# Ternary weights turned by a transposing DMA, and their scales spread over the partitions through a line in DRAM

## What is computed

```
q    = x + braak_embed[stage][..., None]            # (16, 256, 256)
attn = softmax(einsum('bsd,btd->bst', q, f))
y    = einsum('bst,btd->bsd', attn, f)              # the kernel uses attn @ (f @ H)
xh   = y @ H                                        # H: Hadamard, 256 x 256
s    = clip(max|xh| over a row, 1e-05) / 7
xq   = clip(round(xh / s), -8, 7) * s
ws   = clip(mean|weight| over a row, 1e-05)         # one scale for each of 256 outputs
tern = +1 where weight/ws > 0.5, -1 where < -0.5, else 0
out  = x + einsum('bsi,oi->bso', xq, tern * ws)
```

## Time and profile before

| | |
|---|---|
| median of 3 runs | 108.36 us (107.94 to 108.78) |
| the profiled execution: its time | 108.61 us |
| its span in the trace | 106.8 us |
| mean granted clock of PE | 0.97 |
| PE busy | 97.4 us, 91% |
| DVE busy | 87.7 us, 82% |
| ACT busy | 76.1 us, 71% |
| POOL busy | 47.1 us, 44% |
| DMA queue of SP and ACT, share of 16 engines | 45.1% |

### The profile page before, as it was taken

How to read it: one execution, slowest core, us unless ns; L and a number is a source line. 1 busy time by engine, 2 the same in 40 slices (tenths; PEclk the granted TensorE clock), 3 DMA queues, 4 the chain that set the end, 5 groups by cost and what they waited for, 6 DMA issues and landing times.

```text
span 106.8 us, 2584 instructions
## 1 busy us (share of the span) xinstructions
PE 97.4 (91%) x799; PEld 90.9 (85%) x799; DVE 87.7 (82%) x216; ACT 76.1 (71%) x200; POOL 47.1 (44%) x66
## 2 busy tenths in 40 slices
PE   5969899999999999999999999999999998995640
PEld 2439799899999999999999999999999998995410
DVE  1085699798989898989989898989898989699880
ACT  3255986969696978787878787878788865780610
POOL 5034699404343435343435353535353534058050
PEclk9999999999999999999999999999999999999855
DMA  3984632425253664947282728282722222202214
GB/s 68 256 298 120 257 112 30 169 53 199 49 173 134 175 215 119 228 111 237 96 227 86 245 68 262 54 289 49 292 51 98 49 98 49 98 0 98 98 53 143
DMA packets 14850, 14.71 MB, mean 138 GB/s; under 512 B 8054, under 2 KB 8956, under 8 KB 14844
## 3 DMA queue, kind: packets, MB, share of 16 engines
q1 hardware_dynamic: 14688, 14.62, 45.1%
q10 hardware_dynamic: 156, 0.01, 0.1%
HBM read 8.73 MB, written 4.19 MB: 121 GB/s over the span
## 4 chain that ended last, share of the span: by engine, by line
PE 72%; DVE 14%; ACT 4%; DMA 3%; issue 3%; ACTq 1%; DVEq 0%
PE score_bank L461 19%; PE xh_bank L461 18%; PE fh_bank L461 12%; PE prob_bank L450 6%; PE out_bank L516 5%; PE f_bank L450 5%; PE q_bank L450 5%; DMA stage_of<-itok_dram 3%; ACT prob L672 2%; DVE prob_lo L841 1%; DVE least_scale L863 1%; DVE fh_lo L841 1%; DVE raw_scale L819 1%; DVE xh_bank L996 1%; DVE result L1002 1%
## 5 line engine op out<-in xcount | busy, mean ns | idle before, releaser
L359 POOL TENSOR_TENSOR result<-scaled,x_all 128x512 f32<-128x512 f32 x13 | 16.7, 1281 | 24.3 <-DVE scaled L827 24.3
L351 POOL TENSOR_TENSOR code<-code,magic 128x512 bf16<-128x512 f32 x13 | 13.5, 1040 | 14.8 <-ACT code L650 14.8
L650 ACT ACTIVATE code<-xh_bank,inv_scale 128x256 f32<-128x256 f32 x30 | 12.8, 486 | 4.8 <-DVE inv_scale L953 2.8
L672 ACT ACTIVATE prob<-score_bank,neg_max 128x256 f32<-128x256 f32 x32 | 15.0, 478 | 0.9 <-DVE neg_max L868 0.9
L841 DVE TENSOR_TENSOR prob_lo<-prob_bank,prob_hi 128x512 fp32r<-128x512 f32 x16 | 11.1, 691 | 5.2 <-ACT prob_hi L662 5.2
L666 ACT CAST fh_hi<-fh_bank 128x512 fp32r<-128x512 f32 x16 | 9.4, 589 | 7.9 <-PE fh_bank L461 7.7
L461 PE MATMUL score_bank<-f_hi,q_hi 128*128 128x256 f32 x64 | 14.1, 302 | 0.3 <-ACT prob L672 0.3
L461 PE MATMUL fh_bank<-had,f_hi 128*128 128x256 f32 x64 | 14.0, 299 | 0.0
L641 ACT CAST f_hi<-f_bank 128x512 fp32r<-128x512 f32 x15 | 8.8, 587 | 5.7 <-PE f_bank L450 5.7
L461 PE MATMUL score_bank<-f_lo,q_hi 128*128 128x256 f32 x64 | 12.8, 282 | 0.0
L461 PE MATMUL score_bank<-f_hi,q_lo 128*128 128x256 f32 x64 | 12.8, 282 | 0.0
(11 more groups left out here) (129 smaller groups left out, 232.5 us busy)
## 6 DMA issues: line engine op xcount, KB each, us to landing
f_nat<-f_dram SPq DMA_DIRECT2D x16, 256.0 KB, 2.8
x_all<-x_dram SPq DMA_DIRECT2D x16, 256.0 KB, 3.0
out_dram<-result SPq DMA_DIRECT2D x14, 256.0 KB, 2.0
out_dram<-result SPq DMA_DIRECT2D x4, 128.0 KB, 1.8
w_raw<-weight_dram SPq DMA_DIRECT2D x1, 256.0 KB, 4.8
code_t<-code SPq DMA_TRANSPOSE x13, 2.5
had_block<-hadamard_dram SPq DMA_DIRECT2D x1, 64.0 KB, 3.9
embed_sb<-embed_dram ACTq DMA_DIRECT2D x1, 6.0 KB
```

The source lines that it names most:

```text
L351: nc.gpsimd.tensor_tensor(as_rows(code16[:, b.k]), as_rows(code), magic[:, :].broadcast_to([P, W]), ALU.subtract).then_inc(code16_ready, 1)
L359: nc.gpsimd.tensor_tensor(result[:, b.k], as_rows(scaled[:, b.k]), x_all[:, b.at], ALU.add).then_inc(result_ready, 1)
L650: return nc.scalar.activation(to[:, t], xh[:, t], ACT.Copy, bias=MAGIC, scale=inv_scale[:, b.k, t:t + 1])
L672: a = nc.scalar.activation(prob[:, t], score_bank[:, t], ACT.Exp, bias=neg_max[:, b.k, t:t + 1], accum_out=row_sum[:, b.k, t:t + 1])
```

## The change

Both ways of the weight over PE are removed, and with them `ones`, `w_diag`, the two DVE copies and the four waits around them. In their place:

- `tern` is stored by POOL in the order chunk, tile, column, so that one transposing DMA (128 x 512, bf16, as for the codes) gives `tern_t`. POOL still does it in one instruction; its output now goes to four runs of 128 elements.
- `w_scale` (128 x 2, fp32) is stored to a line of 256 elements in DRAM, element by element, and SP waits for its landing; a second DMA then reads the line into all 128 partitions as `w_scale_row`.
- All three stand in SP's queue in front of its step 3, that is behind the loads of batch 4, and in front of the loads of batch 5 and of the turning of the codes of batch 0.
- PE waits for `tern_t` before its step 4 as before, no longer for the row; DVE waits for the row before its step 4.

```
 @@ SP
+            def weight_row():
+                sp.wait_ge(w_scale_ready, 1)
+                sp.dma_start(w_scale_line.rearrange("(t p) -> p t", p=P), w_scale[:, :],
+                             allow_slow_non_contiguous=True
+                             ).then_inc(line_stored, 16)
+                sp.wait_ge(line_stored, 16)
+                sp.dma_start(w_scale_row[:, :], w_scale_line.partition_broadcast(P)
+                             ).then_inc(row_ready, 16)
+
+            def turn_weights():
+                sp.wait_ge(tern_ready, 1)
+                sp.dma_start_transpose(tern_t[:, :, :].rearrange("p c (t s) -> p (c t) s", t=T),
+                                       tern[:, :, :, :].rearrange("p c t d -> p (c t d)")
+                                       ).then_inc(tern_t_ready, 16)
+
             for i in range(B + LAG_STORE - 2):
+                if i == LAG_QUANT:
+                    weight_row()
+                    turn_weights()
                 step(peeled(i), dma_turns=i - LAG_QUANT < turned_by_dma)
 @@ POOL
-            nc.gpsimd.memset(ones[:, :], 1.0).then_inc(ones_ready, 1)
...
-                nc.gpsimd.tensor_tensor(tern[:, :, :], w_pos[:, :, :], w_neg[:, :, :], ALU.subtract
-                                        ).then_inc(tern_ready, 1)
+                nc.gpsimd.tensor_tensor(tern[:, :, :, :].rearrange("p c t d -> p t c d"),
+                                        w_pos[:, :, :].rearrange("p t (c d) -> p t c d", c=C),
+                                        w_neg[:, :, :].rearrange("p t (c d) -> p t c d", c=C),
+                                        ALU.subtract).then_inc(tern_ready, 1)
 @@ PE
-            def weights():
-                pe.wait_ge(tern_ready, 1)
-                for c in range(C):
-                    for t in range(T):
-                        pe.transpose(tern_half[:, c, t * P:(t + 1) * P],
-                                     tern[:, t, c * P:(c + 1) * P], ident16[:, :])
-                pe.wait_ge(diag_ready, 1)
-                pe.wait_ge(ones_ready, 1)
-                for t in range(T):
-                    mm = pe.matmul(out_bank[:, 0, t * P:(t + 1) * P], ones[:, :], w_diag[:, t],
-                                   start=True, stop=True)
-                mm.then_inc(weights_in_bank, 1)
...
-                    if stage == times_hadamard:
-                        weights()
                     stage(b)
-            pe.wait_ge(tern_t_ready, 1)
-            pe.wait_ge(row_ready, 1)
+            pe.wait_ge(tern_t_ready, 16)
 @@ ACT
-            act.wait_ge(w_scale_ready, 1)
-            for t in range(T):
-                a = nc.scalar.activation(w_diag[:, t], ident[:, :], ACT.Copy, scale=w_scale[:, t:t + 1])
-            a.then_inc(diag_ready, 1)
 @@ DVE
-            def weight_copies():
-                dve.wait_ge(weights_in_bank, 1)
-                nc.vector.tensor_copy(tern_t[:, :, :], tern_half).then_inc(tern_t_ready, 1)
-                nc.vector.tensor_copy(w_scale_row[:, :], out_bank[:, 0]).then_inc(row_ready, 1)
...
-                    if stage == split_fh:
-                        weight_copies()
                     stage(b)
+            dve.wait_ge(row_ready, 16)
             for i in range(4, 2 * LOOP_FROM):
```

More of the change, by code:

```diff
@@ L71, in adaln_ffn_kernel @@
         warm = sb("warm", [P, W], BF16)
-        ones = sb("ones", [P, P], F32)
         had_block = sb("had_block", [P, P], F32)
@@ L82, in adaln_ffn_kernel @@
         w_pos = sb("w_pos", [P, T, D], F32)
-        tern = sb("tern", [P, T, D], BF16)
+        tern = sb("tern", [P, C, T, P], BF16)
         tern_t = sb("tern_t", [P, C, O], BF16)
-        w_diag = sb("w_diag", [P, T, P], F32)
         w_scale_row = sb("w_scale_row", [P, O], F32)
+        w_scale_line = nc.dram_tensor("w_scale_line", [O], F32, kind="Internal").ap()
         stage_of = sb("stage_of", [P, B], I32)
@@ L133, in adaln_ffn_kernel @@
         out_bank = bank("out_bank", [P, T, O], F32)
-        tern_half = out_bank[:, T - 1].bitcast(BF16).rearrange("p (c o) -> p c o", c=C)
         last_xh_banks = [f_bank, q_bank]
@@ L171, in adaln_ffn_kernel @@
         bias_ready = sem("bias_ready")
-        ones_ready = sem("ones_ready")
         had_ready = sem("had_ready")
@@ L179, in adaln_ffn_kernel @@
         tern_t_ready = sem("tern_t_ready")
-        diag_ready = sem("diag_ready")
-        weights_in_bank = sem("weights_in_bank")
+        line_stored = sem("line_stored")
         row_ready = sem("row_ready")
@@ L401, in _ @@
             pool.wait_ge(third_last_scaled, 1)
-            pool.wait_ge(row_ready, 1)
+            pool.wait_ge(row_ready, 16)
             nc.gpsimd.tensor_tensor(scaled[:, third_last.k], scaled[:, third_last.k],
```

## The result

The changed kernel takes 115.11 us in the median of 5 runs (112.92 to 115.22), against 108.36 before. The ratio is 1.0496, 95% interval 1.043 to 1.0562: slower by 5%, where no change was forecast. (Some executions of either kernel run about 1.3 us longer at a lower granted clock; ratios leave those out, so this one rests on two of the five, of 114.42 and 112.92 us.) The profiled execution is the one of 114.42 us, with a span of 112.6, so the span has grown by 5.8 us.

The account below looks back on a forecast made before the run. PE, gapless from 21.6 to 88 us, was taken as the bound, its start set by a chain ending in prob_lo. Terms of 0 for PE, ACT, DVE, POOL and SP gave 108.4 us, range 107.6 to 109.2.

Parts of the forecast that it names:

- weight_row: Scale line's store and broadcast on SP: line lands 14.7 to 17.1 us, row by 18.8 to 21.2; no cost.
- turn_weights: DMA turning of tern on SP: issued at 18.6 us, tern_t lands 21.0 to 22.2, before PE asks at 23.05.
- The cover of 5.9 us: On SP before tern is ready: the line's store may take up to 5.9 us without delaying the queue.
- the DRAM line is slow: Rival, SP's queue: line beyond 5.9 us eventually delays tern_t; 8 us gives about 108.5 to 109.6; chance 0.02.
- the gap of 1.05 us: PE's idle time before mix of batch 1, expected to grow from 0.40 to 1.05 us without lowering the clock.
- my estimate of four such blocks in a row: Turning of tern by the skill page's figure: 5.2 us, landing at 23.8, PE gap 0.8 us; 109.2 us, chance 0.02.
- the codes behind two loads: Batch 0's codes on SP, right behind f(5) and x(5): landing 23.2 to 24.4 us, before PE asks at 25.80.
- the stall of `raw_scale` goes: Rival on DVE: raw_scale gets in before POOL's tern, chain 0.97 us shorter; 107.4 us, chance 0.03.

Follow-up runs that it names:

- Another queue: The changed kernel with packed store and broadcast on ACT's queue, SP only turning tern, DVE's wait at scale_out: 112.52 us, ratio 1.0375.
- the turning alone: The kernel before with only tern turned by DMA in SP's queue, the scales staying on PE: 108.16 us, ratio 0.9972.
- the row alone: The kernel before with only the scales sent through the DRAM line by SP, tern still turned by PE: 112.83 us, ratio 1.0367.
- the four stores: The kernel before with four extra stores of w_scale to DRAM from SP's queue, in different piece layouts, waited for only at the end: one execution, 118.56 us.

## Why the prediction was wrong

The forecast 108.4, range 107.6 to 109.2, missed 115.1.

- **The step that failed** is the landing of the line in `weight_row`: "between 12.3 + 2.4 = 14.7 and 12.3 + 4.8 = 17.1". It took 7.5 us (8.3 to 10.1 in others), and the wait for it held the turning back by 1.8 us. With it failed the landing of `tern_t` in `turn_weights`, "18.6 + 2.4 to 3.6": it took 5.6. The first alone would have stayed within what `tern_t` had to spare; the two together made PE idle 2.81 us. The bounds came from transfers with small pieces, but in none of them did two pieces share 8 bytes of DRAM: the transposing DMAs and the broadcast of `itok` write to SBUF, and the stores of before write long rows. No row was like it, and I took the slowest load as the end of a range that had no upper end. The cover of 5.9 us is borne out as far as runs go: with 4.3 us (pieces of 8 bytes) there is no loss, with 7.5 SP was late by 1.8. That the piece size of the store is the cause is shown, by the run with pieces of 8 bytes, which mends both landings (4.3 and 2.8 us). By what way the turning became slow is open, as said under "Another queue".
- **The rival** "the DRAM line is slow" named the mechanism and had a chance of 0.02 and a price that was too low, 109.6 for 8 us. Two things were missing in its price. `tern_t` was still taken to land in 2.4 to 3.6 us, with a cover of its own; by that price 7.5 us for the line would have cost at most 0.7. And the clock: I asked whether the gap of 1.05 us would lower it (gaps of 0.79 to 1.13 us did not), but set no price on it for any rival with a gap. It cost 1.6 us in the trace. A small part of the miss is no fault of the sum: the forecast is compared with a median of 115.1, and 1.1 us of the traced execution come from its start.
- **Right:** PE, ACT and DVE gain nothing from what is taken off them: the gap in front of `mix` of batch 1 grew to 0.87 (0.79 with the turning alone), released by `prob_lo`. POOL's `tern` in four runs takes 1.28 us, as before. `raw_scale` was held again, for 900 ns. The turning by itself lands in time. The Trainium skill, "VectorE: DVE Perf Modes", section "The three transpose paths", has 1309 ns for one 128 x 128 block by DMA; my estimate of four such blocks in a row, by which it would have been 0.8 us late, did not come true (2.5 us for the whole 128 x 512). That the codes behind two loads would still land in time also held: 3.4 us with the turning alone.
- **Half right:** "the stall of `raw_scale` goes" was priced at 107.4; made to happen, with the turning by DMA, it gave 107.26. That nothing in the change would make it happen was right.

## What to carry to other kernels

A transfer's bytes don't bound its time: a store of 1 KB whose neighbouring pieces shared 8 bytes was another kind of transfer here, which took 7.5 to 10.1 us and delayed others, from SP's queue and from ACT's. If no row of a trace shows the kind of transfer that a change brings in, its upper end is open and belongs into the range, with what stands behind it in the queue and what an idle PE costs afterwards. Before small results go to DRAM, look for the order in which each partition's elements lie together, and let the reader take the stride. And where a short operation of one engine is far above its own median, look at what runs beside it: with the turning by DMA in both, moving `tern` took the ratio from 0.9972 to 0.9889, while the work taken off the busiest engine, by itself, had gained nothing clear of noise.

## What was not expected of the hardware

- 256 pieces of 4 bytes took 1.9 us to landing with starts 32 bytes apart, 3.4 with 8, and 7.5 to 10.1 packed; 128 packed ones 8.3. In the change the DMA share is 0.03 while SP waits, so the packets' own records don't show it. Why it is so is not settled; neither is why a broadcast right behind it takes 5.1 to 6.1 us, where it took 4.1 and 4.7 right behind a store of 8-byte pieces and 3.2 to 3.4 by itself.
- A packed store on ACT's queue delayed a transfer that SP issued behind it: a turning's issue took 3.25 us in place of 1.30.
- An idle gap of PE of 2.81 us was followed by about 4 us at granted clock 0.50; with dummy products in the gap it stayed at 1.00. Gaps of 1.86 us (the start of the run with the filled gap), 3.01 (ACT's queue), 3.34 (the row alone) and 5.61 (the four stores) were followed by 0.50 too; after those of 0.79 to 1.21 us, at the start and in front of `mix`, it stayed at 1.00.
